# Attention: probabilities transposed in blocks by DVE and multiplied with V in four 32-row groups of the PE array, instead of 128-row transposes on PE

## The chip, the cores and the metric

The kernel runs on one core of a Trainium2 chip. The metric is device microseconds of one execution, the median of several runs. The core has five engines that work at the same time, each through its own list of instructions in order: PE (TensorE, matrix products), DVE (VectorE), ACT (ScalarE), POOL (GpSimd) and SP (SyncE, here the queue that issues DMAs). They wait for each other through semaphores.

## The reference

A decoder layer for 32 sequences of 112 tokens with 256 features: a state-space mixer with its feed-forward block, then a parallel attention and gated block over a context of 375 rows, then a last feed-forward block. The change is in the middle part:

```
x = layer_norm(x);  context = layer_norm(context)
q = (x @ Wq) * 64**-0.5          # 16 heads of 64
k, v = split(context @ Wkv)      # one head of 64, shared by all 16
sim  = q @ k.T + mask            # per head 112 x 375
attn = softmax(sim)
out  = (attn @ v) @ Wout + (silu(gate) * value) @ W2     # gate, value = x @ W1
x    = x + out;  then layer_norm, relu feed-forward, residual, layer_norm
```

## The kernel before

The mixer runs first (up to about 622 us). Then attention goes through eight groups (`it`) of four sequences. A group has 28 steps (`STEPS`), seven (`NP`) for each sequence: a step handles one pair of 128-row tiles of the 16 x 112 score rows of a sequence, the tiles `e` = 0 and 1 lying on rows 0 to 63 and 64 to 127 of PE's array. The code of each engine is written out by hand as a loop over steps, and each step does, in this order:

- PE: the score pair of step p (`scores`, banks 0 and 1 of PSUM); at two steps of a sequence a batch of probabilities times V (`times_v`, bank 4); the three 128-row transposes of each probability tile of step p-2 (`turn`, banks 2 and 3); then the pieces X and Y that the table `AT` lists for the step.
- DVE: mask and row maximum of step p (`highest`), then reciprocal and scaling of step p-1 (`divide`), norms, then its share of the pieces.
- ACT: head outputs (`heads_out`), copies of the turned tiles of step p-2 (`copies`), exponentials of step p (`exps`), then its share of the pieces.

The pieces are the rest of the layer: "query" (8 tiles), "out" (16 products into each of two tiles), "back" (transposes of the result), "gate" and "value" (8 each), "token" and "ftoken" (transposes of normed tokens), "up", "down" and "kv" (keys and values of the next sequence). A piece writes into one of the banks `MISC` that its `seat` names. PE may not start a piece (`vacant`) before the engine that reads the seat's piece before has emptied it. Before, there are three seats (banks 6, 7, 5): gate, and the even ones of query, back, token, ftoken, up and down, on seat 0, value and the odd ones on seat 1, out and most kv on seat 2.

```
        def vacant(eng, it, piece):
            k, n = seats.before(it, piece)
            if n > 0:
                eng.wait_ge(free[k].sem, n)
            return bank(MISC[k]), full[k].sem
```

A step's scores wait until `highest` has read those of the step before (`hold(pe, h_m, i, 2 * p)`). Group 0 has a table of its own with fewer pieces, and the last group ends in a written-out tail (`early`, `end_out`, `end_back`, `end_turn`, `end_up`, `end_down`).

## Time and profile before

| | |
|---|---|
| median of 3 runs | 1851.41 us (1844.26 to 1853.59) |
| profiled execution, first to last instruction | 1848.1 us |
| PE busy | 1761.8 us, 95% |
| DVE busy | 1310.7 us, 71% |
| ACT busy | 918.7 us, 50% |
| first score pair of attention | at 622.25 us |
| one steady group of attention | 149.74 us |

The profiled execution has no time of its own beside its span, which lies 3.3 us under the median of the runs. A share of busy time is a mean over stages with different limits: the mixer uses all engines, attention mostly PE. The stretches in the section with the rows tell the two apart.

### The profile page before, as it was taken

What the parts mean: (1) busy time and instruction counts of PE and PEld (TensorE: products, weight loads), DVE (VectorE), ACT (ScalarE), POOL (GpSimd) and SP (SyncE); (2) the same over time, 40 slices, a digit from 0 to 9 for tenths busy, and PEclk for the clock granted to TensorE, in tenths of its full rate; (3) what the DMA queues carried; (4) which work ended last, traced back from release to release, by engine and by line L of the source; (5) the groups of instructions that cost most, each with busy time, mean ns of one, the idle gap of its engine ahead of it and who ended that gap; (6) DMA issues with size and microseconds to landing.
All of it is one profiled execution on the core that took longest, in us unless ns stands there. A gap on an engine that the chain in (4) does not pass through costs nothing.

```text
span 1848.1 us, 27947 instructions
## 1 busy us (share of the span) xinstructions
PE 1761.8 (95%) x9224; PEld 1020.1 (55%) x9224; DVE 1310.7 (71%) x3971; ACT 918.7 (50%) x2262; POOL 420.3 (23%) x569
## 2 busy tenths in 40 slices
PE   4579999999999998999999999999999999999997
PEld 2356676766767544455545554544555554555466
DVE  6878988988976588476667648747747666765744
ACT  3444553553541465456545545645645654654542
POOL 4868677777872001000000000000000000000000
PEclk8689999999999999999999999999999999999999
DMA  4000000000013343232222222323223322232200
GB/s 132 11 11 11 21 21 11 31 21 27 6 39 111 95 138 103 55 79 73 73 67 72 76 71 65 81 57 80 66 64 79 75 70 68 72 82 58 54 19 21
DMA packets 102318, 109.22 MB, mean 59 GB/s; under 512 B 38592, under 2 KB 95872, under 8 KB 101280
## 3 DMA queue, kind: packets, MB, share of 16 engines
q1 hardware_dynamic: 101712, 106.99, 21.7%
q8 instruction: 75, 1.23, 0.3%
q14 instruction: 67, 0.55, 0.1%
q10 hardware_dynamic: 464, 0.46, 0.1%
HBM read 96.92 MB, written 7.42 MB: 56 GB/s over the span
## 4 chain that ended last, share of the span: by engine, by line
PE 86%; DVE 8%; ACT 2%; DMA 2%; issue 1%; POOL 1%; DVEq 0%; POOLq 0%; ACTq 0%
PE ps L1530 20%; PE ps L1485 9%; PE ps L1492 9%; PE ps L1523 9%; PE ps L1508 8%; PE ps L314 5%; PE ps L440 4%; PE ps L387 4%; PE ps L427 4%; PE ps L405 3%; PE ps L1590 2%; DVE m_u L727 2%; PE ps L373 2%; PE ps L1584 1%; PE ps L1628 1%
## 5 line engine op out<-in xcount | busy, mean ns | idle before, releaser
L1867 DVE CUSTOM_DVE_ANT_0 x_pr<-ps,x_mk 128x375 f32<-128x375 f32 x448 | 227.6, 545 | 306.1 <-issue 238.9
L1739 ACT ACTIVATE x_pT<-ps 125x384 f32<-125x384 f32 x448 | 195.5, 489 | 269.8 <-PE ps L1492 269.2
L1745 ACT ACTIVATE x_pr<-x_pr,x_mx 128x375 f32<-128x375 f32 x448 | 268.2, 608 | 30.4 <-DVE x_mx L1867 30.4
L1492 PEld LDWEIGHTS ps<-ident,x_pr 128*125 128x125 f32 x1344 | 164.5, 187 | 130.9 <-issue 95.7
L1492 PE MATMUL ps<-ident,x_pr 128*125 128x128 f32 x1344 | 205.7, 289 | 2.5 <-DVE x_pr L1876 2.5
L1530 PE MATMUL ps<-x_xn,x_w 128*128 128x448 f32 x512 | 205.7, 543 | 2.1 <-DVE x_ff L1927 2.1
L1485 PE MATMUL ps<-x_kT,x_qT 64*128 64x375 f32 x896 | 202.6, 529 | 4.1 <-DVE x_mx L1867 4.1
L1876 DVE TENSOR_SCALAR x_pr<-x_pr,x_rc 128x375 f32<-128x375 f32 x448 | 170.9, 424 | 8.0
L1508 PE MATMUL ps<-x_pT,x_va 125*64 125x512 f32 (+1 forms) x768 | 158.4, 548 | 0.6 <-ACT x_pT L1739 0.6
L314 PE MATMUL ps<-m_xa,w_in 128*128 128x448 f32 x352 | 148.2, 568 | 6.2 <-ACT m_xa L532 6.2
L1485 PEld LDWEIGHTS ps<-x_kT,x_qT 64*128 64x128 f32 x896 | 67.7, 185 | 126.3 <-issue 114.4
L1530 PEld LDWEIGHTS ps<-x_xn,x_w 128*128 128x128 f32 x512 | 93.0, 191 | 74.1 <-issue 69.6
L1755 ACT ACTIVATE x_OT<-ps 128x512 f32<-128x512 f32 x64 | 34.9, 545 | 191.6 <-PE ps L1508 191.6
L440 PE MATMUL ps<-fc,m_gl 128*112 128x256 f32 x512 | 113.3, 379 | 0.0
L1530 PE MATMUL ps<-x_xn,x_wq 128*128 128x448 f32 x256 | 105.0, 542 | 0.0
L314 PEld LDWEIGHTS ps<-m_xa,w_in 128*128 128x128 f32 x352 | 67.4, 198 | 65.2 <-issue 56.4
L1508 PEld LDWEIGHTS ps<-x_pT,x_va 125*64 125x64 f32 x768 | 49.4, 136 | 93.7 <-issue 92.9
L440 PEld LDWEIGHTS ps<-fc,m_gl 128*112 128x112 f32 x512 | 89.4, 177 | 19.8 <-issue 1.1
L387 PE MATMUL ps<-m_Lm,m_R 64*16 64x64 f32 (+6 forms) x1792 | 80.6, 241 | 9.5 <-POOL m_R L1012 9.5
L1745 ACT ACTIVATION_READ_ACCUMULATOR x_pr<-x_pr,x_mx 128x1 f32 x448 | 89.3, 199 | 0.0
L1530 PE MATMUL ps<-f_xn,f_w 128*128 128x448 f32 x224 | 88.8, 539 | 0.0
L1523 PE MATMUL ps<-x_OT,x_wo 128*128 128x448 f32 x224 | 88.8, 539 | 0.0
(195 smaller groups left out, 2867.3 us busy)
## 6 DMA issues: line engine op xcount, KB each, us to landing
x_mk<-in_mask SPq DMA_DIRECT2D x224, 187.5 KB, 2.4
x_cx<-in_context SPq DMA_DIRECT2D x32, 375.0 KB
...
```

The costliest lines, as they stand in the source:

```text
L314: last = pe.matmul(to, w_in[:, k, n * 128:(n + 1) * 128], xa[:, k, :], start=(k == 0), stop=(k == KD - 1))
L387: last = pe.matmul(bank(2 * (b % 2) + g)[0:rows, at], Rb[part, c, b, j * S:j * S + rows], Lm[part, c, b * NQ + j, :, :], start=(c == 0), s ...
L440: last = pe.matmul(bank(4 + b // 2)[0:S, (b % 2) * D:(b % 2 + 1) * D], gl[:, k, b * S:(b + 1) * S], fc2[:, k, :], start=(k == 0), stop=(k ...
L1485: pe.matmul(bank(e)[:, 0:J], qT[rows, b, r * ROWS:(r + 1) * ROWS], kT[rows, b % 2, :], start=True, stop=True).then_inc(h_s.sem, 1)
L1492: last = pe.transpose(bank(2 + e)[0:JP, t * ROWS:(t + 1) * ROWS], pr[:, 2 * (p % SLOT) + e, t * JP:(t + 1) * JP], ident[:, :])
L1508: last = pe.matmul(bank(4)[DH * e:DH * e + DH, 0:n * ROWS], va[:, b % 2, t, :], pT[:, k + e:k + 2 * n:2, t, :], start=(t == 0), stop=(t == ...
L1523: last = pe.matmul(to[:, 0:T], lhs, rhs, start=(m == 0), stop=(m == KA + KH - 1))
L1530: last = pe.matmul(to[:, 0:T], weights[:, k, at:at + 128], moving[:, k, :], start=(k == 0), stop=(k == KD - 1))
L1739: act.activation(pT[:, 2 * NV * (batch(p) % 2) + 2 * (p % NP % NV) + e, :, :].rearrange("p t s -> p (t s)"), bank(2 + e)[0:JP, 0:JT * ROWS ...
L1745: act.activation(pr[:, k, :], pr[:, k, :], ACT.Exp, scale=-1.0, bias=mx[:, k:k + 1], accum_out=sums[:, k:k + 1]).then_inc(h_e.sem, 1)
L1867: dve.tensor_tensor_reduce(pr[:, k + e, :], bank(e)[:, 0:J], mk[:, p % SLOT, :], -1.0, 3.0e38, ALU.add, ALU.min, mx[:, k + e:k + e + 1]).t ...
L1876: dve.tensor_scalar(pr[:, k + e, :], pr[:, k + e, :], rc[:, k + e:k + e + 1], None, ALU.mult).then_inc(h_n.sem, 1)
```

## The change

Probabilities no longer pass through PE to be transposed. DVE transposes each 128 x 384 tile (375 columns and zeros) in blocks of 32 x 32 into a ring `blocks` of nine places (`turn`, now DVE's). What lies in 32-row group a of column block c are then the 32 context rows 32c to 32c+31 for the 32 score rows 32a to 32a+31. V is laid out to fit: `va` holds, in each of the four 32-row groups, all twelve blocks of 32 context rows. `times_v` multiplies the seven tiles of a sequence at once, 12 blocks x 4 row groups x 2 column halves = 96 products of 32 rows, 64 columns and 224 moving columns into banks 2 to 5, in two parts, at steps 1 and 2 of the next sequence right behind the score pair.

Further: the scaling by the reciprocal moves from DVE to ACT (`scaled`, at the start of the next step), the reciprocal moves to the end of DVE's step, ACT's copies of turned tiles are gone, and the head outputs are copied in four pieces per sequence at its step 3. The seats shrink to two (banks 6 and 7): out takes seats 1 and 0, kv seat 0. The tables that place the pieces are new; gate 0 now stands in step 11 with both back pieces, gate and value 5 in step 17 with both ftokens, down 0 in step 25 with both tokens. Several tiles share memory (`so`, `xs` in place of `x2`, `fs`), and the tail is rewritten to suit. The DMAs per sequence stay at eight for V.

```diff
-NV = 4
-NB = 2
 SLOT = 4
-MISC = (6, 7, 5)
+MISC = (6, 7)
 SEATS = len(MISC)
 XB = 2
-RESULT, TOKENS, TOKENS_FIRST, FINAL = (10, 11, 12), (20, 21, 22), (16, 17, 20), {STEPS - 2: (0,), STEPS - 1: (1, 2)}
+RESULT, TOKENS, TOKENS_FIRST, FINAL = (11, 12, 13), (17, 20, 23), (16, 17, 20), {STEPS - 2: (0,), STEPS - 1: (1, 2)}
+BLK = 32
+RB = ROWS // BLK
+JC = 12
+JW = JC * BLK
+AHEAD_BY = 2
+RING = NP + AHEAD_BY
+V_AT, V_TAKEN = (1, 2), 3
+V_BANKS = (2, 3, 4, 5)
+UP_BANKS = (0, 2, 3, 4)
...
+OUT_AT = (0, 0, 3, 3, 4, 5, 5, 6, 6, 7, 7, 7, 8, 9, 10, 10)
+GATE_AT, VALUE_AT = (11, 12, 13, 14, 15, 17, 19, 20), (11, 12, 13, 14, 16, 17, 19, 20)
+UP_AT = (18, 18, 21, 21, 22, 23, 24, 24)
...
     if piece[0] == "out":
-        return 2
-    if piece[0] == "kv":
-        return 2 if piece[1] != 1 else 0
+        return 1 - piece[1]
+    if piece[0] == "kv" or piece[0] == "query" and piece[1] >= QUERIES:
+        return 0
     return piece[-1] % 2
...
-        def turn(i, p):
-            for e in range(2):
-                pe.wait_ge(h_n.sem, h_n.value(i, 2 * p + e + 1))
-                hold(pe, h_c, i, 2 * p + e - 1)
-                for t in range(JT):
-                    last = pe.transpose(bank(2 + e)[0:JP, t * ROWS:(t + 1) * ROWS], pr[:, 2 * (p % SLOT) + e, t * JP:(t + 1) * JP], ident[:, :])
-                last.then_inc(h_t.sem, 1)
-
-        def times_v(i, p):
-            b, r = divmod(p, NP)
-            if r not in (NV - 1, NP - 1):
-                return
-            pe.wait_ge(h_c.sem, h_c.value(i, 2 * p + 2))
-            if r == NV - 1:
+        def times_v(i, b, part):
+
+            if part == 0:
                 pe.wait_ge(l_va[b % 2].sem, l_va[b % 2].value(i, VPARTS * 16 * (b // 2 + 1)))
-                hold(pe, o_c, i, 2 * b)
-            else:
-                pe.wait_ge(o_c.sem, o_c.value(i, 2 * b + 1))
-            n, k = r % NV + 1, 2 * NV * (batch(p) % 2)
-            for t in range(JT):
-                for e in range(2):
-                    last = pe.matmul(bank(4)[DH * e:DH * e + DH, 0:n * ROWS], va[:, b % 2, t, :], pT[:, k + e:k + 2 * n:2, t, :],
-                                     start=(t == 0), stop=(t == JT - 1))
-            last.then_inc(h_o.sem, 1)
+                pe.wait_ge(h_t.sem, h_t.value(i, 2 * NP * (b + 1)))
+                hold(pe, o_c, i, RB * b)
+            places = slice(AHEAD_BY * (b % 2), AHEAD_BY * (b % 2) + NP)
+            for c in range(JC // len(V_AT) * part, JC // len(V_AT) * (part + 1)):
+                for a in range(RB):
+                    rows = slice(BLK * a, BLK * a + BLK)
+                    for e in range(2):
+                        last = pe.matmul(bank(V_BANKS[a])[DH * e:DH * e + DH, 0:NP * BLK], va[rows, b % 2, c, :], blocks[rows, places, e, c, :],
+                                         start=(c == 0), stop=(c == JC - 1))
+            if part == len(V_AT) - 1:
+                last.then_inc(h_o.sem, 1)
...
             for p in range(STEPS):
-                if p == 0 and not first:
-                    turn(*back(it, p, 2))
                 scores(it, p)
                 if first and p == 6:
                     result_taken(LAST)
-                if p >= 3 or not first:
-                    times_v(*back(it, p, 3))
-                if p >= 2 or (p == 1 and not first):
-                    turn(*back(it, p, 2))
+                if p % NP in V_AT and (p >= NP or not first):
+                    i, at = back(it, p, NP)
+                    times_v(i, at // NP, V_AT.index(p % NP))
                 parts(it, p, "X", first, last)
                 parts(it, p, "Y", first, last)
...
-        def copies(i, p):
-            for e in range(2):
-                u = 2 * p + e
-                act.wait_ge(h_t.sem, h_t.value(i, u + 1))
-                if e == 0 and p % NP % NV == 0:
-                    hold(act, h_o, i, batch(p) - 1)
-                act.activation(pT[:, 2 * NV * (batch(p) % 2) + 2 * (p % NP % NV) + e, :, :].rearrange("p t s -> p (t s)"), bank(2 + e)[0:JP, 0:JT * ROWS], ACT.Copy).then_inc(h_c.sem, 1)
-
         def exps(i, p):
             for e in range(2):
                 k = 2 * (p % SLOT) + e
                 act.wait_ge(h_m.sem, h_m.value(i, 2 * p + e + 1))
-                act.activation(pr[:, k, :], pr[:, k, :], ACT.Exp, scale=-1.0, bias=mx[:, k:k + 1], accum_out=sums[:, k:k + 1]).then_inc(h_e.sem, 1)
-
-        def heads_out(i, p):
-
-            b, r = divmod(p, NP)
-            if r == 3 and b == 0 and i >= 2:
-                filled(act, i - 1, ("out", KD - 1, 3))
-            if r in (3, NP - 1):
-                at, n = (0, 4 * ROWS) if r == 3 else (4 * ROWS, (NP - 4) * ROWS)
-                act.wait_ge(h_o.sem, h_o.value(i, batch(p) + 1))
-                act.activation(OT[:, i % 2, b, at:at + n], bank(4)[:, 0:n], ACT.Copy).then_inc(o_c.sem, 1)
+                act.activation(pr[:, k, 0:J], pr[:, k, 0:J], ACT.Exp, scale=-1.0, bias=mx[:, k:k + 1], accum_out=sums[:, k:k + 1]).then_inc(h_e.sem, 1)
+
+        def scaled(i, p):
+            k = 2 * (p % SLOT)
+            act.wait_ge(h_r.sem, h_r.value(i, p + 1))
+            for e in range(2):
+                act.activation(pr[:, k + e, 0:J], pr[:, k + e, 0:J], ACT.Copy, scale=rc[:, k + e:k + e + 1]).then_inc(h_n.sem, 1)
+
+        def heads_out(i, b):
+
+            if b == 0 and i >= 2:
+                filled(act, i - 1, ("out", KD - 1, KA - 1))
+            act.wait_ge(h_o.sem, h_o.value(i, b + 1))
+            for a in range(RB):
+                act.activation(OT[i % 2][:, b, :].rearrange("p (r a x) -> p r a x", a=RB, x=BLK)[:, :, a, :],
+                               bank(V_BANKS[a])[:, 0:NP * BLK].rearrange("p (r x) -> p r x", x=BLK), ACT.Copy).then_inc(o_c.sem, 1)
...
             for p in range(STEPS):
-                if p >= 3 or not first:
-                    heads_out(*back(it, p, 3))
-                if p >= 2 or not first:
-                    copies(*back(it, p, 2))
+                if p >= 1 or not first:
+                    scaled(*back(it, p, 1))
                 exps(it, p)
+                if p % NP == V_TAKEN and (p >= NP or not first):
+                    i, at = back(it, p, NP)
+                    heads_out(i, at // NP)
...
         def divide(i, p):
             k = 2 * (p % SLOT)
             dve.wait_ge(h_e.sem, h_e.value(i, 2 * p + 2))
             dve.reciprocal(rc[:, k:k + 2], sums[:, k:k + 2]).then_inc(h_r.sem, 1)
-            dve.wait_ge(h_r.sem, h_r.value(i, p + 1))
+
+        def turn(i, p):
+
+            if p % NP == AHEAD_BY:
+                hold(dve, h_o, i, p // NP)
             for e in range(2):
-                dve.tensor_scalar(pr[:, k + e, :], pr[:, k + e, :], rc[:, k + e:k + e + 1], None, ALU.mult).then_inc(h_n.sem, 1)
+                dve.wait_ge(h_n.sem, h_n.value(i, 2 * p + e + 1))
+                dve.transpose(blocks[:, place_of(p), e, :, :].rearrange("p c x -> p (c x)"), pr[:, 2 * (p % SLOT) + e, :]).then_inc(h_t.sem, 1)
...
                 highest(it, p)
                 if p >= 1 or not first:
-                    divide(*back(it, p, 1))
+                    turn(*back(it, p, 1))
...
                     final_norm(it - 1, stage)
-
-        dve.memset(vT[DH:2 * DH, :, JP:ROWS], 0.0)
+                divide(it, p)
```

The order of the instructions shows what this makes of PE's list. At the back pieces of a steady group, PE's list of before (L1485 are scores, L1492 the transposes, L1508 V, L1552 back, L1530 gate and value, L1590 kv):

```order
L1485 MATMUL ps<-x_kT,x_qT 128x375 x2
L1508 MATMUL ps<-x_pT,x_va 64x384 x6
L1492 MATMUL ps<-ident,x_pr 125x128 x6
L1552 MATMUL ps<-ident,x_oT 112x128 x8
L1485 MATMUL ps<-x_kT,x_qT 128x375 x2
L1492 MATMUL ps<-ident,x_pr 125x128 x6
L1530 MATMUL ps<-x_xn,x_w_125 128x448 x4
L1485 MATMUL ps<-x_kT,x_qT 128x375 x2
```

And the same place now, steps 11 and 12 (L1499 scores, L1559 back, L1537 gate and value, L1597 kv):

```order
L1499 MATMUL ps<-x_kT,x_qT 128x375 x2
L1559 MATMUL ps<-ident,x_oT 112x128 x4
L1537 MATMUL ps<-x_xn,x_w_125 128x448 x2
L1559 MATMUL ps<-ident,x_oT 112x128 x4
L1537 MATMUL ps<-x_xn,x_w_125 128x448 x2
L1499 MATMUL ps<-x_kT,x_qT 128x375 x2
L1597 MATMUL ps<-x_cT,x_wkv 128x375 x2
L1537 MATMUL ps<-x_xn,x_w_125 128x448 x4
```

Back and gate of one seat now follow each other within a step, twice, and in the next step kv and gate 1 do, all on seat 0. DVE's list at the same step 11 (L1858 maximum, L1872 block transposes, L1885 context product, L1942 back, L1923 gate, L1927 value, L1864 reciprocal):

```order
L1858 ISA x_pr,x_mx<-ps,x_mk 128x375
...
L1858 ISA x_pr,x_mx<-ps,x_mk 128x375
...
L1872 STREAM_TRANSPOSE x_blk<-x_pr 128x384 x2
L1885 TENSOR_TENSOR x_cT<-x_cT,x_rb 128x375 x2
L1942 TENSOR_TENSOR x_so<-ps,X 112x512
L1923 SCALAR_TENSOR_TENSOR x_ff<-x_th,ps 128x448
L1942 TENSOR_TENSOR x_so<-ps,X 112x512
L1927 TENSOR_TENSOR x_ff<-x_ff,ps 128x448
...
L1864 RECIPROCAL x_rc<-x_sum 128x2
```

The reader of back 0 stands behind five operations of the step's own scores and the context; the reciprocal closes the step. ACT's list at step 17 (L1738 scaling, L1732 exponentials, L1746 head outputs, L1771 ftoken, L1768 tanh of the gate):

```order
L1738 ACTIVATE x_pr<-x_pr,x_rc 128x375 x2
L1732 ACTIVATE x_pr,x_sum<-x_pr,x_mx 128x375 x2
L1746 ACTIVATE x_OT_131<-ps 128x7x32 x4
L1771 ACTIVATE f_xn<-ps 128x448
L1768 ACTIVATE x_th<-ps 128x448
L1771 ACTIVATE f_xn<-ps 128x448
```

The copy that frees seat 0 after ftoken 0 stands behind eight others; before, both ftokens stood alone in their step behind two copies and two exponentials.

## Rows read from the trace of the kernel before

**Rows 1.** The cores: span and mean granted clock.

```profile
core 0: 1848.1 us, clock 0.979
```

**Rows 2.** Stretches: length, each engine's busy us (instructions), clock, DMA.

```profile
622.25:746.70 124.45, 115.86 (x523) 61.42 (x523) 95.11 (x337) 71.41 (x195) 5.44 (x1) 0.97 0.40 113
1046.18:1195.92 149.74, 149.68 (x642) 76.72 (x641) 99.04 (x371) 80.41 (x215) 0.00 (x0) 1.00 0.28 71
```

**Rows 3.** Time line, PE: start, us, line, output<-inputs, shapes.

```profile
1125.71 0.90 PE L1485 MATMUL ps<-x_kT,x_qT 64*128 64x375 f32 x4
1126.54 0.92 PE L1492 MATMUL ps<-ident,x_pr 128*125 128x128 f32 x6
1127.30 3.17 PE L1530 MATMUL ps<-x_xn,x_w 128*128 128x448 f32 x8
1130.40 0.90 PE L1485 MATMUL ps<-x_kT,x_qT 64*128 64x375 f32 x4
...
1768.54 2.16 PE L1508 MATMUL ps<-x_pT,x_va 125*64 125x384 f32 x12
1770.63 0.92 PE L1492 MATMUL ps<-ident,x_pr 128*125 128x128 f32 x6
...
1802.58 3.19 PE L1628 MATMUL ps<-x_ff,x_w 128*128 128x224 f32 x16
1805.61 0.82 PE L1492 MATMUL ps<-ident,x_pr 128*125 128x128 f32 x6
```

**Rows 4.** The page's groups: weight loads for V, busy and mean ns.

```profile
L1508 PEld LDWEIGHTS ps<-x_pT,x_va 125*64 125x64 f32 x768 | 49.4, 136 | 93.7 <-issue 92.9
```

**Rows 5.** Time line, other engines, steps 25 to 27.

```profile
1178.93 1.34 ACT L1763 ACTIVATE x_xn<-ps,x_cols 128x448 f32<-128x448 f32 x2
...
1180.80 1.00 DVE L1889 TENSOR_TENSOR x_cT<-x_cT,x_rb 128x375 f32<-128x375 f32 x2
...
1186.74 0.62 DVE L1934 TENSOR_SCALAR x_vT<-ps,x_kvb 64x375 f32<-64x375 f32 x1
1186.80 0.56 ACT L1788 ACTIVATE x_kT<-ps,x_kvb 64x375 f32<-64x375 f32 x1
...
1187.39 0.57 DVE L1940 STREAM_TRANSPOSE x_vT<-x_vT 64x384 f32<-64x384 f32 x1
1187.39 0.57 ACT L1790 ACTIVATE x_kT<-ps,x_kvb 64x375 f32<-64x375 f32 x1
...
1187.99 1.41 DVE L1161 BATCH_NORM_STATS2 x_bn<-f_so 112x6 f32<-112x256 f32 x4
```

**Rows 6.** Time line, DVE and ACT, step 14.

```profile
1126.74 0.55 DVE L1867 CUSTOM_DVE_ANT_0 x_pr<-ps,x_mk 128x375 f32<-128x375 f32 x1 [0.30 <-PE ps L1485]
...
1127.88 0.74 DVE L1876 TENSOR_SCALAR x_pr<-x_pr,x_rc 128x375 f32<-128x375 f32 x2
1127.93 0.61 ACT L1745 ACTIVATE x_pr<-x_pr,x_mx 128x375 f32<-128x375 f32 x1
...
1129.11 0.54 ACT L1776 ACTIVATE x_th<-ps 128x448 f32<-128x448 f32 x1
...
1129.74 0.60 DVE L1927 SCALAR_TENSOR_TENSOR x_ff<-x_th,ps 128x448 f32<-128x448 f32 x1
...
1130.51 0.62 DVE L1931 TENSOR_TENSOR x_ff<-x_ff,ps 128x448 f32<-128x448 f32 x1 [0.17 <-PE ps L1530]
```

**Rows 7.** Groups by form: DVE's back product, ACT's nearest forms.

```profile
L1944 DVE TENSOR_TENSOR x_so<-ps,X 112x512 f32<-112x512 f32 x14 | 9.7, 692 | 10.0 <-PE ps L1552 9.0
...
L526 ACT ACTIVATE m_xs<-m_X,m_rr 112x256 f32<-112x256 f32 x32 | 13.6, 500 | 2.3 <-DVE m_rr L77 2.3
...
L1818 ACT ACTIVATE x_oT<-ps 128x224 f32<-128x224 f32 x4 | 1.4, 354 | 5.2 <-PE ps L1628 5.2
```

**Rows 8.** Stretches around two waits of PE at 698 to 703 us.

```profile
697.60:701.40 3.80, 0.63 (x4) 0.40 (x3) 3.56 (x9) 0.98 (x2) 2.27 (x1) 1.00 0.67 120
701.40:708.30 6.90, 5.46 (x11) 2.31 (x12) 5.58 (x17) 1.84 (x5) 0.00 (x0) 0.51 0.19 53
```

More of the change, by code:

```diff
@@ L1068, in schedule @@
     at = {(p, s): [] for p in range(STEPS) for s in "XY"}
[L1069 to L1071 removed]
+    for n in range(QUERIES, KA):
+        at[n - QUERIES, "X"].append(("query", n))
+    for n, p in enumerate(OUT_AT):
+        at[p, "Y"].append(("out", n // KA, n % KA))
     for n, s in enumerate("XY"):
[L1073 removed]
+        at[11, s].append(("back", n))
+        at[17, s].append(("ftoken", n))
+        at[25 + n, "Y"].append(("down", n))
+        at[25, s].append(("token", n))
     for f in range(KH):
[L1075 to L1080 removed]
+        at[GATE_AT[f], "X"].append(("gate", f))
+        at[VALUE_AT[f], "Y"].append(("value", f))
     for n in range(KH):
[L1082 removed]
+        at[UP_AT[n], "Y"].append(("up", n))
     for b in range(GB):
         at[(b - 1) % GB * NP + NP - 2, "X"].insert(0, ("kv", b))
[L1085 to L1087 removed]
+    for n in range(QUERIES):
+        at[STEPS - 1 - (n == 0), "Y"].append(("query", n))
     return at
@@ L1399, in group @@
             for p in range(STEPS):
-                if p == 12 and not first and not last:
+                if p == 13 and not first and not last:
                     sp.wait_ge(o_s.sem, o_s.value(it, 0))
@@ L1658, in end_up @@
                     pe.wait_ge(h_m.sem, h_m.value(NG - 1, U))
-                if h == 0 and n == 2:
-                    pe.wait_ge(h_c.sem, h_c.value(NG - 1, U))
-                if KH * h + n >= 4:
-                    pe.wait_ge(t_hq.sem, t_hq.value(h, n - 3))
+                if h == 0 and n == 1:
+                    pe.wait_ge(o_c.sem, o_c.value(NG - 1, RB * GB))
+                if KH * h + n >= len(UP_BANKS):
+                    pe.wait_ge(t_hq.sem, t_hq.value(h, n + 1 - len(UP_BANKS)))
                 for k in range(KD):
-                    last = pe.matmul(bank(n % 4)[:, 0:TH], fw1[:, k, n * 128:(n + 1) * 128], half(fxn[:, k, :], h), start=(k == 0), stop=(k == KD - 1))
+                    last = pe.matmul(bank(UP_BANKS[n % len(UP_BANKS)])[:, 0:TH], fw1[:, k, n * 128:(n + 1) * 128], half(fxn[:, k, :], h), start=(k == 0), stop=(k == KD - 1))
                 last.then_inc(t_up.sem, 1)
@@ L1821, in end_turned @@
             act.wait_ge(t_ft.sem, t_ft.value(h, 1))
-            act.activation(half(fxn[:, :, :], h), bank((6, 5)[h])[:, 0:KD * TH].rearrange("p (k t) -> p k t", k=KD), ACT.Copy).then_inc(t_fx.sem, 1)
+            act.activation(half(fxn[:, :, :], h), bank(6)[:, 0:KD * TH].rearrange("p (k t) -> p k t", k=KD), ACT.Copy).then_inc(t_fx.sem, 1)
         def end_up(h, n0, n1):
```

198 lines of the change are left out of this document (88 added, 110 removed).

## Prediction

> **What bounds the kernel now.** I read span and clock first, then the stretches, then the time line of single steps, and last the waits that the trace already knows. The whole span is 1848.1 us, with TensorE's clock at its upper level (2.4 GHz) nearly throughout [rows 1]. The stretches show where this change acts: one steady group of four sequences (28 steps) takes 149.74 us, and PE is busy for 149.68 of them, DVE for 99.0, ACT for 80.4; the first group of attention, 124.45 us, leaves PE idle for 8.6 [rows 2]. Six such steady groups stand behind each other, so until now every PE nanosecond in them is a nanosecond of the kernel, and no wait of DVE or ACT costs anything. The reader should keep both halves of that in mind: the change takes work from PE, and it puts DVE and ACT into a loop that was not there.
>
> **What PE loses and gains.** One step of the time line goes: score pair (1125.71), six transposes (1126.54), eight passes of 448 columns (1127.30), next score pair (1130.40), 4.69 us in all [rows 3]. Each fp32 matmul is two passes. The transposes hold PE for 0.76 us; what follows the scores then has its first weight load uncovered instead of them, for which I leave 0.10, an estimate: two score passes of 0.32 each take 0.83 with their entry. So 0.66 us go per step, 28 x 0.66 = 18.5 us per group.
>
> V times probabilities costs two batches per sequence now: the one of 384 columns lasts from 1768.54 to 1770.63, 2.09 us [rows 3], the one of 512 by its columns some 2.7, together 4.8 us. After, each half is 48 matmuls of 32 rows, 64 output columns and 224 moving columns, 96 passes on 8 places of the array (4 row groups x 2 column halves). How many of these run at once is not in the trace; it shows two at once and no more: 12 passes of 384 columns in 2.09 us on two column halves, 0.174 each, where a pass of 448 alone takes 3.10/8 = 0.38, so 384 would be 0.33; and four score passes of 375 columns on two row groups in 0.83 [rows 3]. Row groups and column halves each overlap fully, so I take it that they do so together. A pass of 224 columns is 3.03/16 = 0.19 us (1802.58 to 1805.61). With eight at once a half is 12 x 0.19 + 0.15 for entry and exit = 2.43 us, the pair 4.86. The bounds: two at once 48 x 0.19 = 9.1 us a half; four at once 4.6; weights loaded strictly one by one, 49.4/768 = 0.064 us each [rows 4], 96 x 0.064 = 6.1. Nothing suggests less than 2.3. I take 2.43, the value nearest to what both kinds of overlap show.
>
> So PE has 18.5 - 4 x 0.05 = 18.3 us less to do per group: 131.4 instead of 149.7.
>
> The Trainium skill (TensorEngine Tiling (Array Packing), Performance Considerations) speaks against many short matmuls: each carries some 60 cycles. By that a half would be 96 x 25 ns = 2.4 us of issue alone, level with its streaming, and if the two do not fully overlap some 0.1 to 0.2 us more, an estimate of about 10 us over 64 halves. The trace has no stream this dense, so no row decides it, and the sum goes without it.
>
> **What DVE and ACT gain.** DVE drops two scalings (0.66 us a pair, 1127.88 row) and gets two block transposes of 384 columns. The one of before takes 0.57 and holds the engine for 0.60 (1187.39 to 1187.99); it has 64 partitions, the new one 128 [rows 5]. Below: 0.60 as columns set it; above: 1.2 if partitions counted. Operations on 375 columns cost alike with 64 and with 128 partitions (0.62 and 0.55 us on DVE, 0.56 and 0.61 on ACT) [rows 5, 6], so 0.60, 1.2 us a pair. ACT drops two copies and gets two scalings from SBUF: the nearest row with a scale per partition is 0.50 us for 256 columns [rows 7], the exponential, with its sum read out behind it, 0.61 for 375 [rows 6]; I take 0.5 us from one to the next, bounds 0.4 and 0.6. Both engines stay under PE as sums (about 110 and 86 of 131 us per group).
>
> The sums do not decide, though. Divide now stands at the end of DVE's step, scaling at the start of ACT's next, block transposes behind DVE's next score maximum. From a reciprocal at time T: scalings T+0.2 to 1.2, exponentials to 2.4, tanh to 3.0, DVE gate product to 3.7, value product 4.3, next reciprocal: 4.3 us against PE's 4.03 (4.69 - 0.66) in a gate-and-value step [rows 6]. That alone is small. Worse is that the banks for everything else shrink from three to two, and some steps give PE two pieces in a row with the same bank (bank 6 for even seats). PE then stands until the first has been read out, by an engine with the step's scores ahead of it.
>
> **The waits, step by step** (times from the step's first score pass; DVE starts at 1.03, 1125.71 to 1126.74 [rows 3, 6]; 0.1 from an engine's end to PE is an estimate).
> Maximum and reciprocal last 1.14 (1126.74 to 1127.88), the reciprocal about 0.2 of it, the maximum 0.94.
> - Step 11: back 0, then gate 0. DVE: maximum 0.94, block transposes 1.2, context product 0.95 (two in 1.00 with their tail [rows 5]), back product 0.69 [rows 7], out at 4.8; PE could have gone on at 1.45 and does at 4.9: 3.4 us. Gate 0 to 6.4, back 1 to 6.9; value 0 waits for DVE's gate and back 1 products, out at 8.7: 1.8. Sum 5.2.
> - Step 12: kv, then gate 1. DVE comes late from statistics behind step 11, so scalings start at 2.4, exponentials end at 4.6, two key copies (0.56 and 0.57 [rows 5]) at 5.8; PE ready at 2.2: 3.7.
> - Steps 13 and 14: the loop above, with the context's statistics in 14 (three such as the four of 1.41 us at 1187.99, some 1.2): 1.7.
> - Step 17: feed-forward token 0, then gate 5, same bank. ACT: scalings, exponentials to 3.7, four head copies of 224 columns (one alone 0.35 [rows 7], overlapping about 0.25 each) 1.0, token copy to 5.3; PE ready at 1.4: 3.9; token 1 and value 5: 0.9. Sum 4.8.
> - Step 19: kv, gate 6: 2.1. Step 21: up 2 behind gate 7 on a late DVE: 1.2. Step 25: down 0 behind token 0's copy (1.34 for two, 1178.93 [rows 5]): 2.5. Steps 26, 27: query 0 behind kv: 0.8.
> Total 22.0 us per group, against 18.3 saved: +3.7. What the same pieces did before: back alone in step 9, tokens alone in 18 and 24, kv in a third bank; hidden, since PE is idle for 0.06 us in a group [rows 2].
>
> **Sum**, on the profiled span of 1848.1:
> - six steady groups: 6 x 3.7 = +22
> - first group: light steps fall to the loop's 2.6 to 3.7 us instead of 2.1 to 3.2, heavy ones gain 0.66: -2
> - last group: steps to 22 save 15 and wait 18.7, +3.7; from there to the end about -3.5, since turning and copying of the last probabilities fall out of the closing chain: 0
> - clock: before, after 3.8 us in which PE was busy for 0.63, it ran for 6.9 us at a granted 0.51, the lower level [rows 8]. The group now has three waits of 3.4 to 3.9 us. Each such event would cost at most half of PE's 5.5 busy us, 2.7; most waits have work around them and I count only two events in all: +5
> 1848.1 + 22 - 2 + 0 + 5 = 1873 us of span. The median of the runs (1851.4) is 3.3 above the profiled span, so 1876.
>
> **Rivals.**
> - A, faster. The waits are shorter than worked out, because PE catches up or the pieces are read sooner; PE's 18.3 us count. Place: steps 11, 12, 17, 19, 25. If all waits vanished: 1851 - 8 x 18.3 = 1705. It decides from the point where a group's waits fall under 18.3; at two thirds of mine (14.7) each group gains 3.6 and the kernel ends near 1825. For it: PE waits for nothing now. Against: order of pieces and seats is fixed, and DVE's row of work ahead of the read-out is summed from measured rows. 0.22.
> - B, the eight places do not run together. Four at once: 64 x 2.2 = +140, about 2010; one-by-one weight loads: 64 x 3.7 = +235, about 2110; two at once: +430, about 2300. For it: no row shows more than two. The Trainium skill (TensorE: Matmul & The Clock Gate, Packing small matmuls) reports sixteen places with 10.6 times the throughput, which speaks against it. 0.12.
> - C, the clock falls in most of the 21 long waits: 21 x 2.7 = +57, about 1925. Rows show it once for a longer hollow [rows 8]. 0.13.
> - D, the forecast: waits of 18 to 26 us per group, the gain of PE eaten: 1845 to 1900. 0.53.
>
> **Numbers.** 0.5% (9 us) is about what a measurement of this kernel tells from no change, so faster is under 1842 and slower over 1861. A lies almost wholly in faster; of D a quarter lies within 0.5%; B and C are slower. Faster 0.22, same 0.15, slower 0.63. Range for eight in ten: from A's milder half (1835) to C (1945); it leaves out A's strong end and B. D alone: 1845 to 1900.
>
> **What would show it.** In the profile after: no transposes in the steps; V passes, 96 to a half, in 2.4 us from first to next; PE's busy sum down by about 18 us per group, its waits up from 0.06 to about 22, named as DVE's back product (step 11), ACT's key copies (12, 19) and token copies (17, 25); group length near 153.5. A half much over 2.5 us means B; a granted clock under 1 inside the steady groups means C; a group under 149.7 with waits under 18 means A. The prediction is wrong most easily in the waits, each being a difference of two sums.

## The result, and the profile after

The changed kernel takes 1919.46 us (median of 4 runs, 1917.54 to 1921.14), the one before 1851.82 (4 runs). The ratio is 1.0378, 95% interval 1.0355 to 1.0401: slower by 3.8%. The forecast was 1876 us, range 1835 to 1945: the sign and the range hold, the size does not, +68 us where +25 were forecast. The profiled execution spans 1915.2 us, 67.1 more than before [rows 1].

The cores, after, and the stretches after. Columns: from and to, length, busy us and instructions of PE, its weight loads, DVE, ACT, POOL, granted clock (the share of 2.4 GHz that TensorE was given), DMA share, GB/s.

```profile
core 0: 1915.2 us, clock 0.945
```

```profile
623.15:745.08 121.93, 99.73 (x854) 51.18 (x853) 99.30 (x338) 78.45 (x201) 5.38 (x1) 0.90 0.48 124
745.08:902.74 157.66, 139.35 (x1145) 71.11 (x1145) 102.69 (x362) 87.22 (x223) 0.00 (x0) 0.96 0.31 71
1063.14:1223.56 160.42, 141.32 (x1145) 71.70 (x1145) 104.70 (x372) 87.71 (x223) 0.00 (x0) 0.95 0.32 74
...
1704.86:1863.68 158.82, 143.60 (x1180) 77.97 (x1180) 92.42 (x315) 83.68 (x213) 0.00 (x0) 0.96 0.26 58
...
1127.02:1137.71 10.69, 7.26 (x18) 2.99 (x17) 5.94 (x19) 3.86 (x9) 0.00 (x0) 0.84 0.37 83
1157.33:1161.19 3.86, 1.44 (x9) 0.69 (x8) 3.53 (x11) 3.22 (x12) 0.00 (x0) 1.00 0.68 160
1161.19:1171.43 10.24, 8.88 (x16) 3.68 (x16) 2.02 (x9) 2.42 (x6) 0.00 (x0) 0.50 0.10 32
```

The first four rows are groups 0, 1, 3 and 7. The third stands against the second of [rows 2]: the steady group grew from 149.74 to 160.42 us. It holds 19.10 us in which PE is idle, where there were 0.06, and PE's busy time fell by 8.4 us only, where 18.3 were forecast. And the clock, 1.00 in every steady group before, is 0.95 (0.96 in groups 1 and 7). The last three rows say where: step 12 (1127.02 to 1137.71) has a mean clock of 0.84; in step 17, 3.86 us at the upper level are followed by 10.24 us at the lower one, 1.2 GHz.

PE's waits in that group: engine, line waited for, total us, times, longest.

```profile
PE ps L1537 <- ACT x_kT L1782: 6.0, 3, 3.4
PE ps L1537 <- DVE x_so L1942: 4.5, 2, 3.1
PE ps L1537 <- ACT f_xn L1771: 3.8, 2, 3.2
PE ps L1591 <- ACT x_xn L1755: 2.4, 1, 2.4
PE ps L1537 <- DVE x_ff L1923: 2.2, 2, 1.4
```

These are the waits that the prediction named, with the readers it named: key copies (steps 12, 19, 26), back products (11), ftoken copies (17), the token copy (25), the gate loop (14, 21). Step 17 on the time line, as in [rows 3]:

```profile
1158.16 0.60 PE L1544 MATMUL ps<-ident,x_so 112*128 112x112 f32 x4
...
1159.30 1.03 DVE L1872 STREAM_TRANSPOSE x_blk<-x_pr 128x384 f32<-128x384 f32 x2
...
1160.37 1.07 ACT L1746 ACTIVATE x_OT<-ps 128x224 f32<-128x224 f32 x4
1161.32 0.55 ACT L1771 ACTIVATE f_xn<-ps 128x448 f32<-128x448 f32 x1
...
1161.92 3.35 PE L1537 MATMUL ps<-x_xn,x_w 128*128 128x448 f32 x4 [3.15 <-ACT f_xn L1771]
```

After ftoken 0, PE stands for 3.15 us, until ACT has done the head copies and then the copy that frees the seat. The gate's four passes behind it then take 3.35 us; at the upper level four such passes take 1.77.

The span's 67.1 us by stretches: the start of attention +0.9; group 0 -2.5 (121.93 against 124.45); groups 1 to 6 +61.3 (959.78 from their first score passes to those of group 7, against 898.44); group 7 up to its last scores +8.4 (158.82 against 150.43); from there to the end -1.0.

### The profile page after: what moved, and what is told of

Read it like the earlier page. It is cut to its first block, busy times and chain, and to the rows that moved or that the text cites. A ratio compares the mean times of both kernels' runs of the same rounds, so it can differ in the third digit from the quotient of the medians.

```text
span 1915.2 us, 35558 instructions
## 1 busy us (share of the span) xinstructions
PE 1686.1 (88%) x13256; PEld 975.4 (51%) x13256; DVE 1356.0 (71%) x3972; ACT 977.1 (51%) x2326; POOL 420.0 (22%) x569
## 4 chain that ended last, share of the span: by engine, by line
PE 66%; DVE 18%; ACT 9%; issue 4%; DMA 2%; POOL 1%; DVEq 0%; ACTq 0%; POOLq 0%
PE ps L1537 19%; PE ps L1528 9%; PE ps L1512 8%; PE ps L1499 7%; PE ps L314 4%; PE ps L387 3%; PE ps L405 3%; ACT x_pr L1732 3%; PE ps L427 3%; DVE m_u L727 2%; PE ps L440 2%; ACT x_pr L1738 2%; DVE m_rs L759 2%; PE ps L373 2%; DVE x_blk L1872 1%
## 5 line engine op out<-in xcount | busy, mean ns | idle before, releaser
L1858 DVE CUSTOM_DVE_ANT_0 x_pr<-ps,x_mk 128x375 f32<-128x375 f32 x448 | 227.0, 544 | 233.2 <-PE ps L1499 143.9
L1738 ACT ACTIVATE x_pr<-x_pr,x_rc 128x375 f32<-128x375 f32 x448 | 247.7, 602 | 272.4 <-DVE x_rc L1864 272.4
L1537 PE MATMUL ps<-x_xn,x_w 128*128 128x448 f32 x512 | 250.5, 630 | 110.4 <-ACT x_kT L1782 37.8
L1732 ACT ACTIVATE x_pr<-x_pr,x_mx 128x375 f32<-128x375 f32 x448 | 267.5, 599 | 85.5 <-DVE x_mx L1858 85.3
L1872 DVE STREAM_TRANSPOSE x_blk<-x_pr 128x384 f32<-128x384 f32 x448 | 232.0, 557 | 1.7 <-ACT x_pr L1738 1.4
L1499 PE MATMUL ps<-x_kT,x_qT 64*128 64x375 f32 x896 | 210.1, 546 | 11.2 <-DVE x_mx L1858 9.5
L1537 PEld LDWEIGHTS ps<-x_xn,x_w 128*128 128x128 f32 x512 | 100.9, 212 | 221.7 <-issue 88.5
L1512 PE MATMUL ps<-x_blk,x_va 32*64 32x224 f32 x6144 | 162.6, 354 | 0.2
L1512 PEld LDWEIGHTS ps<-x_blk,x_va 32*64 32x64 f32 x6144 | 132.8, 132 | 38.6 <-issue 33.9
L1499 PEld LDWEIGHTS ps<-x_kT,x_qT 64*128 64x128 f32 x896 | 70.4, 191 | 160.4 <-issue 138.1
L1537 PE MATMUL ps<-x_xn,x_wq 128*128 128x448 f32 x256 | 111.5, 563 | 8.0 <-ACT x_kT L1782 7.3
L1923 DVE SCALAR_TENSOR_TENSOR x_ff<-x_th,ps 128x448 f32<-128x448 f32 x64 | 39.6, 619 | 94.0 <-ACT x_th L1768 93.4
L314 PEld LDWEIGHTS ps<-m_xa,w_in 128*128 128x128 f32 x352 | 67.1, 197 | 64.7 <-issue 55.9
L1537 PE MATMUL ps<-f_xn,f_w 128*128 128x448 f32 x224 | 93.5, 555 | 4.8 <-DVE x_ff L1923 4.8
L1528 PE MATMUL ps<-x_ff,x_w 128*128 128x448 f32 x224 | 89.5, 542 | 0.0
L427 PE MATMUL ps<-m_xb,fc 128*128 128x448 f32 x224 | 85.3, 539 | 0.0
L1732 ACT ACTIVATION_READ_ACCUMULATOR x_pr<-x_pr,x_mx 128x1 f32 x448 | 85.2, 190 | 0.0
```

Of the source, the lines that this page charges most:

```text
L314: last = pe.matmul(to, w_in[:, k, n * 128:(n + 1) * 128], xa[:, k, :], start=(k == 0), stop=(k == KD - 1))
L427: last = pe.matmul(bank((3, 2, 6)[n % 3])[:, 0:T], fc1[:, k, n * 128:(n + 1) * 128], xb[:, k, :], start=(k == 0), stop=(k == KD - 1))
L1499: pe.matmul(bank(e)[:, 0:J], qT[rows, b, r * ROWS:(r + 1) * ROWS], kT[rows, b % 2, :], start=True, stop=True).then_inc(h_s.sem, 1)
L1512: last = pe.matmul(bank(V_BANKS[a])[DH * e:DH * e + DH, 0:NP * BLK], va[rows, b % 2, c, :], blocks[rows, places, e, c, :], start=(c == 0), ...
L1528: last = pe.matmul(to[:, 0:T], lhs, rhs, start=(m == 0), stop=(m == KA + KH - 1))
L1537: last = pe.matmul(to[:, 0:T], weights[:, k, at:at + 128], moving[:, k, :], start=(k == 0), stop=(k == KD - 1))
```

## Experiments

Two theories stood against each other for the missing 43 us. **Theory 1**: the waits are about as long as forecast, and the excess is TensorE's clock, which falls at three of them in most groups. **Theory 2**: the waits themselves are longer than worked out. Theories 3 and up are stated where they come in. Step lengths below are distances between the first score passes of two steps in the trace.

### The waits filled with products that nobody needs: fill3 and fill5

```diff
+FILL = {('gate', 1): (('value', 1), 4, 448), ('gate', 5): (('ftoken', 1), 4, 420), ('down', 0): (('token', 1), 3, 400)}
...
+        def filler(it, piece):
+            mate, products, width = FILL[piece]
+            vacant(pe, it, mate)
+            for n in range(products):
+                pe.matmul(bank(7)[:, 0:width], wq[:, 0, 0:128], wq[:, 1, 0:width], start=True, stop=True)
+
         def part(it, piece):
             kind, n = piece[0], piece[-1]
+            if it >= 1 and piece in FILL and not (it == NG - 1 and FILL[piece][0] in AHEAD):
+                filler(it, piece)
```

This is fill3; fill5 has also `('gate', 0): (('back', 1), 4, 400)` and `('gate', 6): (('value', 6), 2, 448)`.

> The changed kernel with products of constant weights added on PE (written to bank 7, read by nobody): 4 of 448 columns between kv and gate 1 in step 12, 4 of 420 between ftoken 0 and gate 5 in step 17, 3 of 400 ahead of down 0 in step 25, about 3.0, 2.8 and 2.0 us, each a little shorter than the wait that stands there (3.43, 3.15, 2.39). Theory 1 (the excess over the forecast is TensorE's clock: 17 us per group at the lower level, which the three waits bring): the clock stays at its upper level there, the waits vanish as idle time but not as time, and a group falls from 160.4 to about 152, the kernel to about 1855 us, although PE does more work. Theory 2 (the waits themselves are longer than worked out, and the lower clock stands only beside them): the group stays at 160 to 161, the kernel at 1918 to 1930.

> As the run before, with 4 products of 400 columns also between back 0 and gate 0 in step 11 and 2 of 448 between kv and gate 6 in step 19. Theory 1: those two waits lowered the clock nowhere, so nothing more comes of it than safety against another fall: within 3 us of the run with three fillers, 1855 us, granted clock 1.0 through all steady groups. Theory 2: 1918 to 1935. If the run with three fillers shows a new fall in step 11, this one is faster than it by some 3 us per group.

Measured: fill3 1883.75 us, 1.0196 of before (1.0177 to 1.0216); fill5 1869.47, 1.0121 (1.0097 to 1.0144). The changed kernel with work added to PE is 36 and 50 us faster than without (by the ratios, each taken beside the kernel before, by 1.8 and 2.6% of it). A group of fill5, then the stretch from group 1 to the last scores, and below them PE's waits in the group that follows the first:

```profile
897.77:1050.62 152.85, 145.79 (x1179) 74.03 (x1179) 104.72 (x372) 87.38 (x223) 0.00 (x0) 1.00 0.34 78
744.94:1815.20 1070.26, 1022.63 (x8276) 525.16 (x8276) 718.43 (x2531) 607.31 (x1545) 0.00 (x0) 1.00 0.33 75
```

```profile
PE ps L1538 <- DVE x_ff L1932: 2.2, 2, 1.4
PE ps L1538 <- DVE x_so L1951: 1.8, 2, 1.5
PE ps L1538 <- ACT x_kT L1791: 1.5, 3, 0.6
PE ps L1538 <- ACT f_xn L1780: 1.0, 2, 0.7
```

The fillers take the place of idle time and the clock never leaves 1.00 in seven groups. The group is 152.85 us: this is the group of the forecast (149.74 + 3.7) without a fall of the clock. The fillers alone change no step: steps 11 and 19, which are filled too and had no fall in the changed kernel's groups 2 to 6, keep their 9.91 and 7.51 us. Step by step against the changed kernel: step 12 8.99 for 10.69, step 17 9.12 for 12.60, step 18 4.04 for 4.76, step 25 6.07 for 7.73: 7.56 us, all of the 7.57 between 160.42 and 152.85. The clock therefore costs 7.6 us per group with three falls, and theory 2 falls.

fill3 did less than expected (1884 for 1855): its steps 12, 17, 18 and 25 read as in fill5, but the clock now fell in step 11, which is not filled, in each of the seven groups, and in the group from 1055.04 on this step lasts 11.04 us instead of 9.91. In the changed kernel the same wait of 3.06 us lowers the clock in group 1 alone. Step 11 in groups 1 and 3 of the changed kernel, back 0 being done and gate 0 waiting:

```profile
803.60 3.36 PE L1537 MATMUL ps<-x_xn,x_w 128*128 128x448 f32 x4 [3.06 <-DVE x_so L1942]
...
1121.66 1.77 PE L1537 MATMUL ps<-x_xn,x_w 128*128 128x448 f32 x4 [3.06 <-DVE x_so L1942]
```

The wait is the same, and so are the lengths of the eleven steps ahead of it; the passes behind it run at the lower clock once and at the upper one once. So neither the length of a wait nor what PE waits for tells by itself whether the clock falls.

Both runs also missed by the size of the clock's share: the expectations took 8.5 us for it in each of eight groups, and it was 48 us over the seven steady ones (1118.6 us from group 1's first to group 7's last scores in the changed kernel, 1070.3 in fill5).

### One part alone: two seats in the kernel before

```diff
-MISC = (6, 7, 5)
+MISC = (6, 7)
...
 def seat(piece):
     if piece[0] == "out":
-        return 2
-    if piece[0] == "kv":
-        return 2 if piece[1] != 1 else 0
+        return 1 - piece[1]
+    if piece[0] == "kv" or piece[0] == "query" and piece[1] >= QUERIES:
+        return 0
...
-            to = bank(MISC[2])
+            to = bank(MISC[1 - c])
...
-                last.then_inc(full[2].sem, 1)
+                last.then_inc(full[1 - c].sem, 1)
```

> The kernel before with one part of the change alone: the third seat (bank 5) is gone, out takes seats 1 and 0, kv seat 0; all else is as before. Theory 1 (a seat less by itself makes waits where kv and gate 2 or kv and out follow each other in one step): waits of some 2.4 us in steps 5 and 12 and 0.3 to 1 in steps 20, 26 and 27, about 6 us per group, group 155 to 156, kernel 1890 to 1900 with the clock kept, up to 1920 with a fall in each group. Theory 4 (with the longer steps of before and its own table the seat costs nothing; the new table is what does): 1848 to 1860.

Measured: 1906.83 us, 1.0324 (1.0301 to 1.0347). Its group, and PE's waits in it:

```profile
1066.31:1223.78 157.47, 151.89 (x642) 77.33 (x641) 99.03 (x371) 80.40 (x215) 0.00 (x0) 0.99 0.27 68
```

```profile
PE ps L1530 <- ACT x_kT L1790: 3.9, 1, 3.9
PE ps L1523 <- ACT x_kT L1790: 1.7, 1, 1.7
```

Waits in the two steps expected (12 and 5; none in steps 20, 26 and 27), with one fall of the clock in each group: +7.7 us per group. Theory 4 falls. The seat alone, without any of the rest, costs 60 us. That this is near the whole loss of 68 says little: the changed kernel has 19.1 us of waits per group and not 5.6, and PE's shorter work pays part of them back.

### Banks of their own, kind by kind

V leaves banks 2 to 5 empty from a sequence's step 4 to the next one's step 1. These versions let pieces use them; V's first part waits for their readers, and they for V's head copies.

```diff
-MISC = (6, 7)
+MISC = (6, 7, 2, 3, 4)
+OWN = {"back": 2, "ftoken": 2, "token": 2, "kv": 4}
...
-        at[17, s].append(("ftoken", n))
+        at[18, s].append(("ftoken", n))
...
-GATE_AT, VALUE_AT = (11, 12, 13, 14, 15, 17, 19, 20), (11, 12, 13, 14, 16, 17, 19, 20)
-UP_AT = (18, 18, 21, 21, 22, 23, 24, 24)
+GATE_AT, VALUE_AT = (11, 12, 13, 14, 15, 17, 18, 19), (11, 12, 13, 14, 16, 17, 18, 19)
+UP_AT = (20, 20, 21, 21, 22, 23, 24, 24)
...
-def seat(piece):
+def seat(piece, start=False):
...
+    if piece[0] in OWN and not start:
+        return OWN[piece[0]] + (piece[-1] if piece[0] != "kv" else 0)
...
```

own_kv has only "kv" in `OWN`, own_kv_back_token all but "ftoken"; in both the table of steps stays as it was. What the cut leaves out counts the seats and adds the waits just named.

> The changed kernel with kv alone in a bank of its own (bank 4, which V leaves empty from its sequence's step 4 on); back, token and ftoken stay on the shared seats, and nothing moves between steps. Theory 1 (each pair of pieces on one seat is a wait of its own, and the clock's falls hang on the waits): the waits behind kv in steps 12 (3.4 us), 19 (1.9) and 26 (0.6) go, those of 11, 17 and 25 stay as they are: 6 us less idle time per group, group 152 to 155, kernel 1855 to 1878. Theory 3 (DVE and ACT are short of time as a whole there): the idle time turns up again in steps 13, 20 or 27, group 157 to 160, kernel 1895 to 1920.

> As the run before, with back and token in banks 2 and 3 too; of the pairs on one seat only ftoken 0 and gate 5 in step 17 is left. Theory 1: the waits of steps 11 (3.1 and 1.5, of which about 1 stays ahead of value 0 or moves to step 13) and 25 (2.4) go as well: group 143 to 147 with the fall of the clock in step 17, kernel 1795 to 1830. Theory 3: what DVE has to do in steps 11 to 14 fills the place of the waits, group 150 or more, kernel over 1845.

> The changed kernel with back, ftoken and token written to banks 2 and 3 and kv to bank 4, which V leaves empty from its sequence's step 4 on; ftokens move from step 17 to 18, gates and values 6 and 7 from steps 19 and 20 to 18 and 19, up 0 and 1 to step 20. Theory 1 (pieces of one seat behind each other are the waits, and the waits are the low clock): the waits of steps 11, 12, 17, 19 and 25 go, some 18 us per group, and with them all falls of the clock; what is left is PE's work of 132 us and the loop of scaling, exponentials and gate of about 2, a group of 134 to 137 us, kernel 1740 to 1760. Theory 3 (DVE and ACT with their new loop are the bound, and the seats only show where PE stands): the waits turn up in other steps, a group of 145 to 152, kernel 1815 to 1865.

Measured: own_kv 1870.71 us, 1.0096 (1.0071 to 1.0121); own_kv_back_token 1823.83, 0.9839 (0.9811 to 0.9867); own_banks 1760.07, 0.9536 (0.9506 to 0.9567), which beats both kernels. One group of each, in this order:

```profile
1049.24:1202.40 153.16, 138.73 (x1145) 70.45 (x1145) 104.46 (x372) 87.53 (x223) 0.00 (x0) 0.96 0.35 78
```

```profile
1040.15:1186.88 146.73, 136.26 (x1145) 69.69 (x1145) 104.37 (x372) 87.57 (x223) 0.00 (x0) 0.97 0.37 81
```

```profile
1016.55:1154.22 137.67, 131.88 (x1144) 68.06 (x1145) 104.21 (x372) 87.20 (x223) 0.00 (x0) 1.00 0.37 87
878.88:1016.55 137.67, 133.50 (x1145) 68.81 (x1145) 104.41 (x372) 87.21 (x223) 0.00 (x0) 0.99 0.38 86
```

Idle time of PE goes 19.1, 14.4, 10.5, 5.8 as pairs on one seat are taken away, with DVE's and ACT's work unchanged. The first two lie in the ranges of theory 1, the third at or just over their ends (137.67 for 134 to 137, 1760.07 for 1740 to 1760). Theory 3 holds for a part: of what is taken away, some turns up in step 13, where PE is idle for 0.03 us in the changed kernel and for 1.3, 3.2 and 2.8 in the three versions. The falls of the clock go down but not away: own_banks still has one, in step 13, in five of its seven groups. The last version also moves pieces between steps, and no run has its banks without its table, so what the move alone does is not shown. The third version's PE is busy for 131.88 us at full clock; the prediction had 131.4. PE's waits in the group at 1016.55:

```profile
PE ps L1553 <- DVE x_ff L1941: 3.7, 3, 2.0
PE ps L1515 <- issue: 1.2, 1, 1.2
PE ps L1515 <- DVE x_mx L1876: 0.8, 1, 0.8
```

Of its two groups above, one has a fall of the clock (0.99) and the other none, and both last 137.67: in steps 13 and 14, where it falls, PE waits for DVE, and a slower PE has 1.6 us more to do and waits 1.6 us less.

### What is left: DVE's norms and who scales

```diff
-RESULT, TOKENS, TOKENS_FIRST, FINAL = (11, 12, 13), (17, 20, 23), (16, 17, 20), {STEPS - 2: (0,), STEPS - 1: (1, 2)}
+RESULT, TOKENS, TOKENS_FIRST, FINAL = (12, 13, 16), (17, 20, 23), (16, 17, 20), {STEPS - 2: (0,), STEPS - 1: (1, 2)}
```

That is own_spread. own_spread2 has `(13, 16, 17), (20, 23, 24)` in place of the two triples, own_late also the ftokens in step 19. own_scale_dve is own_spread with this:

```diff
             dve.reciprocal(rc[:, k:k + 2], sums[:, k:k + 2]).then_inc(h_r.sem, 1)
+            dve.wait_ge(h_r.sem, h_r.value(i, p + 1))
+            for e in range(2):
+                dve.tensor_scalar(pr[:, k + e, 0:J], pr[:, k + e, 0:J], rc[:, k + e:k + e + 1], None, ALU.mult).then_inc(h_n.sem, 1)
...
-                if p >= 1 or not first:
-                    scaled(*back(it, p, 1))
...
```

> The version with banks of their own, with the stages of the result's norm on DVE in steps 12, 13 and 16 in place of 11, 12 and 13. There, PE waited 2.0 and 0.8 us in step 13 for gate products that stood behind back products, context product and statistics on DVE. Theory 1: this wait goes or falls under 0.8, and with it the fall of the clock that most groups still had there: group 135 to 136 instead of 137.7 (138 to 139 with a fall), kernel 1735 to 1750 instead of 1760. Theory 3 (DVE is short of time in steps 11 to 14 as a whole): the wait moves to step 14 or 16, kernel 1755 to 1765.

> As the run before, with the scaling by the reciprocal back on DVE, behind the reciprocal at the end of the step (two operations, 0.66 us a pair), so that ACT's next step begins with the exponentials. Theory 7 (the wait in step 14 and the small ones of steps 20 and 27 are the loop through ACT's scaling, 4.3 us long): they go, group 133 to 134, kernel 1720 to 1735. Theory 8 (DVE decides: a gate and value step then asks 0.94 + 1.2 + 0.2 + 0.66 + 1.24 = 4.24 us of it, against 4.04 of PE, and 18.5 us more per group): waits grow in steps 11 to 14 and 17 to 19, group 136 to 140, kernel 1745 to 1775.

> The version with all four kinds in banks of their own, with DVE's norms spread further: the result's in steps 13, 16 and 17 (was 11, 12, 13), the tokens' in steps 20, 23 and 24 (was 17, 20, 23). From the durations, DVE then has 5.9, 4.8, 5.0 and 4.8 us to do in steps 11 to 14 (20.5 in all) where PE has 18.2; with the norms in 11 to 13 it was 24.0, and PE idled for 4.2 us there. Theory 9 (DVE's sum over steps 11 to 14 sets this stretch): it shrinks by the difference of 3.5 us less what cannot be moved out, to a group of 134.5 to 136, kernel 1735 to 1750. Theory 7 (the loop through ACT's scaling sets it): idle time stays at 1.4 to 3 us in steps 13 and 14, group 137 to 138, kernel 1757 to 1767.

> The run before, with both ftokens in step 19 instead of 18. There the run before had swapped the 4.2 us of waits in steps 13 and 14 for 4.49 us in step 18, where ftoken 0 waited for the result's norm, applied by DVE at the end of step 17, and a fall of the clock of 3.4 us with it (step 18 10.87 us instead of 4.8). Theory 9 (no other engine's sum stands in the way once the stages are spread): the wait in step 18 goes and with it the fall; left are 0.45 us in step 13 and 1.2 in step 27, a group of 133.5 to 135, kernel 1728 to 1745. Theory 10 (the wait only moves on, since DVE is late through step 19): 1 to 3 us of it appear in step 19 or 20, group 136 to 138, kernel 1750 to 1765.

Measured: own_spread 1766.44 us, 0.9544 (0.9524 to 0.9564); own_spread2 1783.42, 0.9619 (0.9600 to 0.9638); own_late 1763.59, 0.9531 (0.9514 to 0.9547); own_scale_dve 1813.75, 0.9803 (0.9771 to 0.9835). PE's longest waits in a group of own_spread2 and in one of own_late:

```profile
PE ps L1560 <- DVE x_so L1192: 4.5, 1, 4.5
...
PE ps L1553 <- DVE x_ff L1941: 0.5, 1, 0.5
```

```profile
PE ps L1553 <- DVE x_ff L1941: 2.9, 2, 2.5
```

own_spread2 confirms half of theory 9: with the norms out of steps 11 to 14, PE's idle time of 4.2 us in steps 13 and 14 shrinks to 0.6, so DVE's norms set it, and theory 7 as stated falls. DVE's sum and the loop are not fully parted by this, since the norms stand ahead of the reciprocal that starts the loop.

But ftoken 0 then waits 4.5 us for the norm (a group of 139.9 us for the 134.5 to 136 of theory 9), and once it is moved behind that (own_late) PE waits 2.5 us for a gate product in step 18. That one hangs on the loop: DVE's stage of the norm, 2.2 us in step 17, holds back the reciprocal, ACT's scalings, exponentials, head copies and tanh come behind it, and then the gate product. So theory 10 holds for size and sum (137.7 us, 1763.59), though the wait stands in step 18 and not in 19 or 20.

For own_spread theory 3 holds, the kernel being 1.4 us over its range: the idle time of step 13 moves to steps 14 (2.2 us) and 18 (1.0). A residue of 4.2 to 6.5 us per group moves about with DVE's norms, and no version of the four is measurably better than own_banks. A group of own_scale_dve:

```profile
1041.23:1184.47 143.24, 134.20 (x1145) 68.90 (x1145) 124.01 (x428) 59.26 (x167) 0.00 (x0) 0.99 0.37 83
```

DVE's busy time rises by 20 us, the group by 5.4 over own_spread's 137.8; the waits grow to 9.0 us, 7.9 of them in steps 13, 14, 18 and 27. Theory 8 was right in kind and too mild (136 to 140 us and 1745 to 1775 expected). With banks of their own, scaling on ACT and not on DVE is worth 47 us of the kernel.

### What sets a V half: v_pairs and v_columns

```diff
-            for c in range(JC // len(V_AT) * part, JC // len(V_AT) * (part + 1)):
-                for a in range(RB):
+            for pair in range(2):
+              for c in range(JC // len(V_AT) * part, JC // len(V_AT) * (part + 1)):
+                for a in (2 * pair, 2 * pair + 1):
```

v_columns: `places` and the output slice hold 4 tiles instead of `NP` = 7.

> The changed kernel with each V half in another order: the six column blocks of row groups 0 and 1 first, then those of row groups 2 and 3, so that only four places of the array have neighbours to run with; the same 96 passes. Theory 5 (a half is set by moving columns, eight places running together: 12 passes of 0.19 us): the half grows from 2.5 to 4.7 us, steps 1 and 2 from 4.99 to about 7.2. Theory 6 (a half is set by how fast PE starts passes, some 26 ns each, whatever the place): the half stays at 2.5, step 1 at 4.99. Halfway values would mean that both count.

> The changed kernel with V products of 128 moving columns in place of 224 (three of the seven tiles of a sequence are left out of the product, so the output is not the layer's). Theory 5: a half takes 12 x 0.107 + 0.15 = 1.4 us instead of 2.5, step 2 falls from 4.99 to about 3.9 or to what the DVE and ACT loop allows. Theory 6: 96 starts of 26 ns, the half stays at 2.5 us and step 2 at 4.99.

The half of the changed kernel, of v_pairs, and of v_columns:

```profile
1069.51 2.53 PE L1512 MATMUL ps<-x_blk,x_va 32*64 32x224 f32 x96
```

```profile
1121.36 4.09 PE L1513 MATMUL ps<-x_blk,x_va 32*64 32x224 f32 x96
```

```profile
1057.69 1.65 PE L1512 MATMUL ps<-x_blk,x_va 32*64 32x128 f32 x96
```

The kernels took 2039.92 and 1869.03 us, one run each; the readings here are those of the half in the traces. Theory 5 holds, theory 6 falls: columns and the number of places running together set the half. In the changed kernel's trace the eight passes of a round start 6 to 7 ns apart and rounds 0.189 us apart; with 128 columns the rounds are 0.109 us apart. At the upper clock of 2.4 GHz that is 454 and 262 cycles, two for each column. (In the later rounds of v_columns single starts are up to 23 ns apart, the rounds still 0.109 us.) v_pairs, with rounds of four 0.189 us apart, stays under the 4.7 expected because the two halves of its order overlap: from 1.59 to 2.23 us behind the first pass, the last rounds of one pair of row groups and the first of the other run together.

## Why the prediction was right about the direction and wrong about the size

**PE's work: right.** 131.4 us per group forecast, 131.88 measured in own_banks, with the clock up. A V half takes 2.53 us for 2.43 forecast: twelve rounds of 0.189 and 0.26 of entry and exit for 0.15. Rival B is out. The Trainium skill (TensorE: Matmul & The Clock Gate, Packing small matmuls) reports sixteen places running together, with some 4 ns from one start to the next; this trace has eight together, with 6 to 7 ns. The Trainium skill's other rule (TensorEngine Tiling (Array Packing), Performance Considerations) of some 60 cycles a matmul does not show as a floor: v_columns runs 96 passes in 1.65 us, 17 ns each or 41 cycles. The forecast's "about 110" us of DVE work per group does not follow from its own terms (99.0 - 28 x 0.66 + 28 x 1.2 = 114; measured 104.7); nothing else rests on it.

**Waits: right in place and reader, 13% long in sum.** By PE's idle time in the trace, with the forecast in brackets: step 11 4.5 (5.2), 12 3.4 (3.7), 13 and 14 1.4 (1.7), 17 3.8 (4.8), 19 1.9 (2.1), 21 0.8 (1.2), 25 2.4 (2.5), 26 and 27 0.8 (0.8); 19.1 in all (22.0). In step 11 six operations of DVE, and not five, stand ahead of the back product; the forecast's sum had all six. Two block transposes take 0.96 us from the first to the next instruction on DVE (1159.30 to 1160.26), not 1.2; and in step 17 ACT was through with the exponentials 3.0 us behind the first score pass (1157.33 to 1160.37), not 3.7. The sum, which a group without a fall of the clock checks, is +3.1 (fill5) for +3.7 forecast. Two errors of 2 to 3 us make up this near hit: the waits are 2.9 us shorter, but PE's busy time at full clock (152.85 - 19.10 = 133.8) is 2.4 us more than 131.4. In own_banks, with few waits, it is 131.88; that PE loses time beside each wait fits this, but is not isolated.

**The clock: the step that failed.** The prediction counted the falls as rare: "most waits have work around them and I count only two events in all: +5". In the trace the granted clock falls three times in each of groups 2 to 6, for 3.4 us at the wait in step 12, 10.2 in step 17 and 3.4 in step 25, and twice in groups 1 (steps 11 and 25) and 7 (steps 12 and 17). The three cost 1.7, 4.2 and 1.7 us in a group, 7.6, and 48 over the seven groups (fill5). So the term was undersized tenfold: 19 falls and 48 us where two and 5 us were put. With 48 in place of 5 the forecast is 1919; the other terms together are 3 us off (1868.1 us of span without the clock's term, where fill5 spans 1865.0), so that a match to under 1 us is luck. Rival C (each of 21 long waits a fall at 2.7 us, "about 1925", chance 0.13) was in effect what happened, for its mechanism and nearly for its number. Its details differ: it counted the three longest waits of a group (steps 11, 12 and 17), while in five of seven groups the third fall stood at the wait of 2.4 us in step 25 and not in step 11; and a fall cost 1.7 or 4.2 us. The mistake was to price a repeated event as a rare one: [rows 8] showed that the clock does fall after an idle stretch, and steady groups repeat what one of them does (groups 2 to 6 fall alike).

**Group 0: right in sum,** -2.5 for -2; its single steps were not compared. **The last group with its tail: off by the clock.** From group 7's first score pass to the end the kernel takes 210.3 us, against 203.0 before: +7.4 where +3.7 and -3.5 were forecast. In fill5, where the clock holds nearly to the end, the same stretch takes 202.7, 0.2 less than before.

**Rival A** (shorter waits, faster) had a condition that leaves the clock out: it decides under 18.3 us of waits, but own_kv, with 14.4, still has groups of 153.2 us, since the clock falls there too. The order of pieces did not allow it in this kernel; own_kv_back_token, with 10.5, and own_banks, with 5.8, are on its side of the point.

Left open: which waits lower the clock. In the changed kernel 3.06 us of idle time in step 11 did so in group 1 and in no other, and 2.40 in step 25 did so in each of the six groups that have that wait; in fill3 the one in step 11 did in all seven. Length alone does not decide, and no run here isolates what does.
